# A decoder layer with 8 experts: the first expert tile filled from batches 0 to 5 only, its first layer among the routing steps

## What is computed

```python
feats = x.reshape(-1, x.shape[-1])                       # 896 x 256
scores = jax.lax.stop_gradient(feats @ centroids.T)      # 896 x 8
expert = jnp.argmax(scores, axis=1)
alpha = jax.nn.sigmoid(jnp.sum(feats * centroids[expert], axis=-1, keepdims=True))
# an expert: h = normalised xs * g + b;  xs + relu(h @ W1e.T + b1e) @ W2e.T + b2e
y = jnp.einsum('te,etd->td', onehot, ys)
out = alpha * y + (1.0 - alpha) * feats                  # then one more layer norm
```

## Time and profile before

| | |
|---|---|
| three runs | 426.25, 427.77, 428.92 us |
| the profiled execution | 426.72 us, its span 425.0 us |
| TensorE busy | 398.4 us, 94% |
| VectorE busy | 272.8 us, 64% |
| ScalarE busy | 240.8 us, 57% |
| POOL busy | 129.4 us, 30% |
| chain that ended last, by engine | TensorE 57%, VectorE 8%, ScalarE 7%, DMA 2%, POOL 1% |
| last f2 matmuls end, last L997 | 328.4 us |
| first layer of tile 0 starts | 342.2 us |
| first layer of tile 1 follows in the chain | 351.1 us |
| second layer of the last tile ends | 412.7 us |

### The profile page before, as it was taken

The page is one execution under the profiler, slowest core; times in us unless marked ns, Lnnn a source line. Parts: engine busy times, 40 slices in busy tenths (PEclk is TensorE's granted clock), DMA queues, the critical chain, the costliest instruction groups (busy, mean ns, idle before and its releaser), DMA issues.

```text
span 425.0 us, 10535 instructions
## 1 busy us (share of the span) xinstructions
PE 398.4 (94%) x3742; PEld 332.7 (78%) x3742; DVE 272.8 (64%) x944; ACT 240.8 (57%) x810; POOL 129.4 (30%) x259
## 2 busy tenths in 40 slices
PE   8989999999999999999999999999999799998980
PEld 8757787878878878787787888887889689898560
DVE  5577777777667777677776715669777737441620
ACT  0204886699787888898889986767222023324120
POOL 4250115023022231131310303324436503761421
PEclk9999999999999999999999999999999979999996
DMA  7960180610010105100000006920491421997000
GB/s 211 267 199 37 40 228 1 216 38 18 2 38 18 38 2 215 38 17 4 1 2 2 4 2 245 433 114 2 187 422 37 139 63 37 376 382 285 26 28 18
DMA packets 11561, 47.10 MB, mean 111 GB/s; under 512 B 1568, under 2 KB 6272, under 8 KB 9344
## 3 DMA queue, kind: packets, MB, share of 16 engines
q1 hardware_dynamic: 9040, 31.92, 21.9%
q0 software_dynamic: 1920, 12.35, 7.8%
q10 hardware_dynamic: 544, 2.08, 1.8%
HBM read 41.44 MB, written 4.91 MB: 109 GB/s over the span
## 4 chain that ended last, share of the span: by engine, by line
PE 57%; DVE 8%; ACT 7%; DMA 2%; issue 2%; POOL 1%; DVEq 0%; POOLq 0%; ACTq 0%
PE bank_pt L701 9%; PE bank_scores L817 6%; PE bank_out L853 5%; PE bank_out L723 5%; PE bank_out L746 5%; PE bank_pt L736 5%; PE bank_out L578 5%; PE bank_out L564 4%; PE bank_scores L685 3%; PE bank_out L571 3%; ACT arena L1286 2%; ACT arena L1297 2%; DMA arena<-expert_rows,slot_expert 2%; DVE arena L1047 1%; PE bank_scores L691 1%
## 5 line engine op out<-in xcount | busy, mean ns | idle before, releaser
L1306 ACT ACTIVATE arena<-bank_pt 125x448 f32<-125x448 f32 (+1 forms) x128 | 66.5, 546 | 34.9 <-PE bank_pt L701 34.8
L1286 ACT ACTIVATE arena<-arena,negmaxc 112x375 f32<-112x375 f32 x128 | 76.6, 604 | 13.6 <-DVE negmaxc L1047 13.2
L1047 DVE CUSTOM_DVE_ANT_0 arena<-bank_scores,arena 112x375 f32<-112x375 f32 x128 | 65.2, 543 | 18.4 <-PE bank_scores L691 12.4
L701 PE MATMUL bank_pt<-ident,arena 112*125 112x112 f32 (+1 forms) x512 | 74.7, 276 | 1.8 <-ACT arena L1306 1.2
L701 PEld LDWEIGHTS bank_pt<-ident,arena 112*125 112x125 f32 (+1 forms) x512 | 63.1, 175 | 15.0 <-ACT arena L1306 5.8
L578 PE MATMUL bank_out<-arena 128*112 128x256 f32 (+1 forms) x224 | 56.5, 383 | 0.1
L1386 POOL TENSOR_TENSOR vareps<-meanvar,scal 112x1 f32<-112x1 f32 (+1 forms) x49 | 9.5, 194 | 121.8 <-DVE meanvar L926 95.1
L1297 ACT ACTIVATE arena<-bank_scores,negmaxs 112x112 f32<-112x112 f32 x128 | 43.3, 353 | 3.4 <-DVE negmaxs L1053 2.8
L1339 ACT ACTIVATE arena<-bank_scores,consts 128x128 f32<-128x128 f32 x64 | 18.3, 369 | 45.5 <-PE bank_scores L817 41.0
L578 PEld LDWEIGHTS bank_out<-arena 128*112 128x112 f32 (+1 forms) x224 | 37.7, 181 | 7.7 <-DVE arena L977 0.5
L564 PE MATMUL bank_out<-arena 128*128 128x112 f32 x320 | 41.2, 282 | 0.2 <-DVE arena L959 0.2
(11 more groups left out here) (186 smaller groups left out, 671.1 us busy)
## 6 DMA issues: line engine op xcount, KB each, us to landing
arena<-moe SPq DMA_DIRECT2D x8, 2048.0 KB, 12.1
arena<-ctxT SPq DMA_DIRECT2D x8, 375.0 KB, 3.1
arena<-mask SPq DMA_DIRECT2D x8, 164.1 KB, 3.4
arena<-x_slots SPq DMA_DIRECT2D x9, 130.0 KB, 2.8
x_slots<-arena SPq DMA_DIRECT2D x8, 130.0 KB, 2.6
arena<-weights SPq DMA_DIRECT2D x1, 1024.0 KB, 5.2
arena<-fi SPq DMA_DIRECT2D x1, 1024.0 KB, 6.7
arena<-fo SPq DMA_DIRECT2D x1, 1024.0 KB, 8.7
```

The lines of the kernel that those rows point to most:

```text
L701: last = nc.tensor.transpose(dst[0:kp, j * S:(j + 1) * S], probs[0:S, (n % 2) * HG + j, c * kp:(c + 1) * kp], ident[0:S, 0:S])
L1047: v.tensor_tensor_reduce(out=probsC[0:S, i % (2 * HG)], in0=score_bank[j][0:S, 0:KX], in1=masks[0:S, u % 2], scale=-1.0, scalar=3.0e38, op ...
L1286: a.activation(probsC[0:S, i % (2 * HG)], probsC[0:S, i % (2 * HG)], ACT.Exp, bias=negmax["c"][0:S, u, at:at + 1], scale=-1.0, accum_out=s ...
L1306: a.activation(probsT[0:kp, n % RT, c], pt_bank[PT[stage, i] % RP][0:kp, 0:HG * S], ACT.Copy).then_inc(pt_free, 1)
```

## The change

Expert 0's tile takes rows of batches 0 to 5 only. After batch 5's ranks are made, a new step `room` raises expert 0's count to 128 if it is below (one 1x1 matmul and two operations on one element). Rows of expert 0 in batches 6 and 7 then rank beyond 128 and go to the mixed tile. The steps `xn` and `se`, the matrices `sel` and all of `WARM` are gone.

What SP reads early is now the whole tile 0. `ei` is two transposes that complete it, and its gain is two ACTIVATEs on ScalarE. New steps in the list are `tot`, the totals matmul, and `first` 0 to 7, the eight column blocks of tile 0's first layer. After the list TensorE starts with tile 0's second layer, then transposes tile 1. SP reads tiles from 1 on, and tile 0's residual comes from the early read.

`place_rest` is split: the places of the rows beyond 128 are made ahead of tile 1's normalisation, the rest (`name_parts`) after tile 0's `add_tile`. POOL sends the first two `x_more` scatters ahead of tile 0's inverse deviation. The late tiles' buffers have other places in the arena, and SP's load of the second biases waits for the last `f2` in place of the last `f1`. Most due times of the tables are changed by a little; of these the diff shows a few lines.

```diff
-FEED = [((0, 1), 33.06), ((2, 3), 37.07), ((4, 5), 42.71), ((6,), 47.72), ((7,), 51.24)]
+FEED = [((0, 1), 33.08), ((2, 3), 37.09), ((4, 5), 42.73), ((6,), 47.74), ((7,), 51.26)]
...
-FIRST_START = (-1.72, -1.37, 0.03, 1.7, 8.88, 13.57, 13.97, 19.51)
+FIRST_START = (-1.72, -1.29, 0.03, 1.76, 8.93, 13.57, 13.97, 19.52)
...
 LATE = 2
-WARM = {("sc", 6): 6, ("rk", 6): 4, ("zx", 7): 4, ("sc", 7): 4, ("rk", 7): 1}
 WARM_FIRST = 6
-HEAD = {"en": (-0.24,), "ei": (-0.24,), "xn": (-0.46, 0.34), "se": (0.14, 0.25)}
-SEND = (41.1, 44.24, 46.59, 50.31, 50.75, 53.25, 55.43, 57.33)
+HEAD = {"en": (0.21,), "ei": (-0.28,), "first": (0.41, 0.45, 0.46, 0.47, 0.48, 0.49, 0.5, 0.51), "tot": (0.39,)}
+SEND = (41.63, 44.43, 46.78, 50.45, 50.94, 53.52, 55.79, 57.94)
...
+    order.insert(min(order.index(("rk", B - LATE - 1)) + 1, order.index(("sc", B - LATE))), ("room", 0))
+    for early, later in ((("sc", B - LATE - 1), ("room", 0)), (("room", 0), ("sc", B - LATE)), (("en", 0), ("ei", 0)), (("ei", 0), ("first", 0)), (("rk", B - 1), ("tot", 0)),
+                         (("f1", FIRST_PIECE[-1] - 1), ("ei", 0)), (("sm", GROUPS - 1), ("ei", 0))):
+        assert order.index(early) < order.index(later), (early, later)
     return order
...
+        total_of = bank[5][:, 384:384 + E]
...
             sp.dma_start(xs_early, x_slots[0:128, :]).then_inc(early_in, 16)
-            sp.wait_ge(hidden_ready, FIRST_PIECE[-1])
+            sp.wait_ge(out_full, OUT["f2", B - 1] + 1)
             sp.dma_start(b2_sb.rearrange("p e d -> p (e d)"), b2rows.to_broadcast([128, E * D])).then_inc(moe_b2_in, 16)
             sp.wait_ge(out_free, N_OUT)
             sp.wait_ge(scattered, 16 * B)
             used = None
-            for t in range(TILES):
+            for t in range(1, TILES):
...
+            def first_layer(t, chunks_of=range(FC)):
+
+                w1 = moe_w[:, EXPERT_AT[t], 0:C * F].rearrange("p (c f) -> p c f", c=C)
+                for f in chunks_of:
+                    for c in range(C):
+                        last = mm(bank[2 * (t % 2) + f // 4][:, f % 4 * 128:(f % 4 + 1) * 128],
+                                  w1[:, c, f * 128:(f + 1) * 128], xsT[:, t % 2, c], start=c == 0, stop=c == C - 1)
+                    if f % 4 == 3:
+                        last.then_inc(t_hid_full, 1)
+
+            def second_layer(t):
+
+                w2 = moe_w[:, EXPERT_AT[t], C * F:].rearrange("p (f d) -> p f d", f=FC)
+                for f in range(FC):
+                    if f % 4 == 0:
+                        pe.wait_ge(t_hid_ready, 2 * t + f // 4 + 1)
+                    last = mm(bank[6 + t % 2][:, 0:D], hidT[:, t % 2, f], w2[:, f], start=f == 0, stop=f == FC - 1)
+                last.then_inc(t_y_full, 1)
+
+            def tile_transposed(j):
+
+                pe.wait_ge(t_normed, j + 1)
+                if j >= 2:
+                    pe.wait_ge(t_xT_ready, j - 1)
+                for c in range(C):
+                    last = nc.tensor.transpose(bank[4 + j % 2][:, c * 128:(c + 1) * 128],
+                                               xsn[:, j % 2, c * 128:(c + 1) * 128], ident[:, :])
+                last.then_inc(t_xT_full, 1)
...
+                elif stage == "room":
+                    pe.wait_ge(counted, 1)
+                    mm(out_slot(slot)[0:1, 0:1], chosen[0:S, B - LATE - 1, 0:1], ones[0:S, 0:1], start=True, stop=True).then_inc(out_full, 1)
                 elif stage == "ei":
-                    assert STEPS.index(("ei", 0)) < STEPS.index(("se", 0))
                     pe.wait_ge(early_normed, 1)
                     pe.wait_ge(probs_ready, PROBS["sm", GROUPS - 1] + HG)
                     for c in range(C):
-                        mm(bank[2 + c][:, 0:128], xsn_early[:, c * 128:(c + 1) * 128], ident[:, :], start=True, stop=False)
-                elif stage == "se":
-                    pe.wait_ge(late_normed, i + 1)
-                    pe.wait_ge(selected, i + 1)
-                    for c in range(C):
-                        last = mm(bank[2 + c][:, 0:128], xsn_late[:, i, c * 128:(c + 1) * 128], sel[i], start=False, stop=i == LATE - 1)
-                    if i == LATE - 1:
-                        last.then_inc(t_xT_full, 1)
-
-                for n in range(WARM.get((stage, i), 0)):
-                    if n == 0:
-                        pe.wait_ge(probs_ready, PROBS["sm", GROUPS - 1] + HG)
-                    mm(bank[0][:, 0:128], ident[:, :], ident[:, :], start=True, stop=True)
+                        last = nc.tensor.transpose(bank[2 + c][:, 0:128], xsn_early[:, c * 128:(c + 1) * 128], ident[:, :])
+                    last.then_inc(t_xT_full, 1)
+                elif stage == "tot":
+                    pe.wait_ge(hidden_ready, FIRST_PIECE[-1])
+                    pe.wait_ge(placed, B)
+                    mm(total_of, ones[0:S, :], chosen[0:S, B - 1], start=True, stop=True).then_inc(totals, 1)
+                elif stage == "first":
+                    if i == 0:
+                        pe.wait_ge(moe_in[0], 16)
+                        pe.wait_ge(t_xT_ready, 1)
+                    first_layer(0, (i,))
 
             pe.wait_ge(out_free, N_OUT)
-            pe.wait_ge(placed, B)
-
-            mm(bank[7][:, 0:E], ones[0:S, :], chosen[0:S, B - 1], start=True, stop=True).then_inc(totals, 1)
-
-
+
+            second_layer(0)
+            tile_transposed(1)
             used = None
-            for t in range(TILES):
+            for t in range(1, TILES):
                 m, halves_of = mixed(t), [bank[2 * (t % 2) + half] for half in range(2)]
 
                 if t == 5:
...
                 j = t + 1
                 if j < TILES:
                     with when_used(pe, used, j):
-
...
+                        tile_transposed(j)
                 with when_used(pe, used, t):
 
-                    if t == 1:
-                        pe.wait_ge(more_placed, 1)
                     if t >= 2:
                         pe.wait_ge(t_y_added, t - 1)
                     if m is None:
...
+                        second_layer(t)
...
-                    if i >= B - LATE:
-                        dve.wait_ge(hidden_ready, EARLY_PIECES)
-                        v.scalar_tensor_tensor(sel[i - B + LATE], slots, ebase[0:S, i:i + 1], rank[0:S, i:i + 1].to_broadcast([S, 128]),
-                                               ALU.subtract, ALU.is_equal).then_inc(selected, 1)
...
+                elif stage == "room":
+
+                    v.tensor_scalar(room[0:1], full(slot)[0:1, 0:1], -1.0, 128.0, ALU.mult, ALU.add).then_inc(out_free, 1)
+                    dve.wait_ge(out_free, slot + 1)
+                    dve.wait_ge(counted, 1)
+                    counts = chosen[0:1, B - LATE - 1, 0:1]
+                    link(v.scalar_tensor_tensor(counts, room[0:1], 0.0, counts, ALU.max, ALU.add))
                 elif stage == "en":
+
                     dve.wait_ge(early_in, 16)
                     v.tensor_scalar(xsn_early, xs_early[:, 0:D], xs_early[:, MEAN:MEAN + 1], xs_early[:, RSTD:RSTD + 1],
                                     ALU.subtract, ALU.mult).then_inc(early_normed, 1)
-                elif stage == "xn":
-                    u = B - LATE + i
-                    dve.wait_ge(hidden_ready, EARLY_PIECES)
-                    dve.wait_ge(x5_rstd, u + 1)
-                    v.tensor_scalar(xsn_late[:, i], xrows[0:S, u, 0:D], xrows[0:S, u, MEAN:MEAN + 1], xrows[0:S, u, RSTD:RSTD + 1],
-                                    ALU.subtract, ALU.mult).then_inc(late_normed, 1)
...
-            gain_tile(0)
-            normalise_tile(0)
+            v.tensor_copy(tile_token[:, 0:1], xs_early[:, TOKEN:TOKEN + 1]).then_inc(t_normed, 1)
+            place_rest()
             normalise_tile(1)
             used = None
             for t in range(TILES + 1):
                 for j, step in ((t, rows_tile), (t + 1, gain_tile), (t + 2, normalise_tile), (t - 1, finish_tile), (t, add_tile)):
-                    if t == 0 and step == add_tile:
-                        place_rest()
                     if t == 5 and step == add_tile:
                         used = parts_used(dve)
                     if 0 <= j < TILES and not (step == rows_tile and mixed(j) is None):
                         with when_used(dve, used, j):
                             step(j)
+                if t == 0:
+                    name_parts()
...
+                elif stage == "ei":
+
+                    act.wait_ge(t_xT_full, 1)
+                    for c in range(C):
+                        last = a.activation(xsT[:, 0, c], bank[2 + c][:, 0:128], ACT.Identity, bias=col("beta", c), scale=col("gamma", c))
+                    last.then_inc(t_xT_ready, 1)
...
             for t in range(E + 1):
                 if t:
                     send(t - 1)
-                inverse_deviation(t, 128, t_stats, t_rstd, t, eps=2)
+                if t:
+                    inverse_deviation(t, 128, t_stats, t_rstd, t, eps=2)
```

(3 more changed lines are left out.)

125 lines of the change are left out of this document (54 added, 71 removed), and 125 rows, old and new, of the table SHIFT.

## The result

The changed kernel takes 422.19 us, the kernel before 428.57 (medians of 20 runs each). The ratio is 0.986, interval 0.984 to 0.989: 5.8 us faster. It leaves out the executions in a slower state, three of the kernel before and two of the changed one, and so differs from the 6.4 us between the medians of all. The profiled execution took 422.64 us with a span of 420.4, where before it was 426.72 and 425.0.

The account below looks back on a forecast made before the run. Bounds: handover from routing to expert tiles, low clock there, mixed tile's parameter wait. Terms +0.2, -3.8, +1.0, -0.05 (second layer without transposes ahead), +1.1 give -1.5 us: 427.77 to 426.3, range 423.7 to 429.0.

Parts of the forecast that it names:

- From the last token_slot to tile 0's first layer: Handover from routing to tile 0: late input products and gain leave the path, 0.55 us in place of 4.37, -3.8.
- The uncovered transposes and gain of tile 1: Behind tile 0's second layer: transposes 0.22, gain and handover 0.88 no longer hidden, +1.1 us.
- The order of VectorE's steps: Last routing steps: copy and scores of batch 6 go ahead of batch 7's zf, at 331.95 instead of 330.95.
- The load of tile 1: Ahead of tile 1: load normalised at 345.6, needed at 348.4, so hidden with 2.8 us to spare.
- The stall at the mixed tile: At place 7: TensorE still stands 1.5 us for the gathered parameters, which land 1.5 us earlier.
- place_rest cost nothing: On VectorE ahead of tile 1's normalisation: place_rest, 4.0 us, is hidden behind tile 1's load.
- A part took 10.0 us ..., part 0 with none ahead of it too: Weight part gathers of later tiles: 10.0 us from issue to landing, carried over unchanged.
- rival of the stall: Mixed tile: gathers wait behind one another, so issued further apart they land sooner and TensorE does not stop; gain 3.0, chance 0.10.
- first layer 6.2 in place of 5.2, +1.0: Tile 0's first layer: 3.7 us plus 2.5 lost over 4.8 us at low clock, against 5.2 before.
- 'placed' +0.2: End of the routing steps: last token_slot at about 338.05 instead of 337.86, net +0.2 us.
- The front decides: Rival: moved steps in the first 325 us shift the time 2 us either way, 424.3 or 428.3; chance 0.15.
- A microsecond won before 351.08 is won at the end, unless something outside TensorE stops it: Expert tiles from tile 1's first layer on: about 7.25 us of TensorE each, so earlier gains carry to the end.

Follow-up runs that it names:

- a_mid: Changed kernel with tile 1's transposes between the fifth and sixth products of tile 0's second layer instead of behind it; ratio 0.982 to the kernel before.
- b_tables: Kernel before with only the changed kernel's due times for all steps up to the routing; ratio 0.998 to the kernel before.

## Why the prediction missed

**Right.** From the last token_slot to tile 0's first layer I forecast 3.8 us less: 3.65 in each of three profiles. The uncovered transposes and gain of tile 1, forecast at 1.1, were 1.13 (348.70 to 349.83), and a_mid took the wait in them away. The order of VectorE's steps made zf of batch 7 come 1.5 later, of which 0.55 was a later f2 and 1.0 the order, as forecast. The load of tile 1 was ready 1.9 us early (2.8 forecast). The stall at the mixed tile stayed (1.5 forecast; 1.28, 2.8 and 1.7 seen). place_rest cost nothing.

**A reading that was wrong.** "A part took 10.0 us ..., part 0 with none ahead of it too": the view gives 10.0 three times because it had the landing of one part only, the last. In the two further profiles of the kernel before all four are there, from 8.7 or 8.8 for the first to 9.9 or 10.5 for the last. And the parameters took 5.3 to 5.7 us with no part ahead, 8.0 to 10.1 behind the parts. So these gathers do hold each other up, against what the prediction held against its rival of the stall; the stall stayed because the parameters still followed the last part by 4.7 us, as before.

**"first layer 6.2 in place of 5.2, +1.0".** This term was mis-sized. The 6.2 rested on 4.8 us at the low clock; it was 3.3, 4.0 and 3.4, and the layer took 5.29, 5.63 and 5.39. And the 5.2 came from one profile, whose low stretch was 6.8 us; in two more it was 10.2, and the layer took 6.75 and 6.16. By the means the term is 5.4 in place of 6.0: -0.6. I took the clock "as low at 338.6" and counted the low time from there, as if it began anew. In fact the fillers' absence moved the fall to between 331 and 333, and the return came earlier with it.

**"'placed' +0.2".** It was +0.8. The missing 0.6 is the same clock: the score and rank matmuls of batch 7 ran at 0.50 (L795 and L796 took 0.54 and 0.39, in the kernel before 0.36 and 0.21), and with the fillers back the term is +0.1. I had put the low clock into the first layer only, although I said it would fall between the routing steps.

**"The front decides", chance 0.15, up to 2 us.** It gave 1.5 us (b_tables 1.7), one dip of the clock near 293 us apart, which took 1.6 back in the very profile I compared with.

**What the sum left out: the end.** "A microsecond won before 351.08 is won at the end, unless something outside TensorE stops it" holds, but the sum ended with the last second layer and took the 12.3 us behind it as fixed. This is the step that failed most: a term put at nothing without a reason. They were 9.5; in the means of three profiles each, the difference is 2.2 us of the tail and 0.4 in front of VectorE's last add, which started 0.48 us behind the matmuls in every profile of the kernels built from before and 0.11 in those of the changed kernel. The cause of the 0.4 was not tested. No rival spoke of the tail. It was in the trace of before: 8.0 us from the last scatter's issue to the end of the span, with the branches in the records, and a change that removes 47 entries from TensorE's queue could move it. That the walk over the unused code sets the tail, and that its length goes with the number of instructions, is shown. That the 2.2 us are missing from the gain once the tails are equal is not: two such pairs still differ by 7.0 and 5.7 us, the first by more at the mixed tile, the second with a stall left in the kernel before. Whether that has to do with the code taken out or is chance, one profile of each can't say.

So of the 4.3 us missed, in the means of three profiles each, 2.2 are the tail, 1.6 less lost in the first layer, 1.0 the front and 0.4 VectorE's add; against them stand 0.6 more lost ahead of placed. The rest, a start 0.6 later and the mixed tile, varies from run to run. Part of the 1.6 is chance: the low stretch of the kernel before was 3.4 us longer in two profiles than in the one that the prediction rests on.

## What to carry over

Read the stretch from the last transfer to the end of the span as its own term: where never-taken code stands at the end of an engine's program, count its long branches in the instruction records, and expect any change in the number of instructions to move them. A cost taken out of both kernels need not shrink their difference by what it was: measure the pair. Take a term that hangs on the granted clock from several profiles, since one shows only one of its lengths. And when a change pulls dense work closer to fillers, try the fillers again before removing them: here neither kept the clock alone, and together they did.

## What the hardware showed that I did not expect

- A jump over code that is not run took 0.21 us mostly and 2.0 to 3.2 us at some places, each long one with a 16384-byte instruction transfer of its own; ten entries more or fewer at the start of a queue of some 4,100 switched one of them at its end.
- With the same order and the same busy time ahead, the clock fell in one profile and not in another. It fell near 293 us in 3 of the 11 profiles with this order. These are the windows of the changed kernel's first and second profile, 3.08 of 4 us busy in both, and then 0.50 against 1.00:

```profile
288.00:292.00 4.00, 3.08 (x43) 2.37 (x42) 3.37 (x13) 2.36 (x11) 2.19 (x6) 1.00 0.00 0
292.00:294.00 2.00, 2.00 (x10) 1.96 (x11) 1.82 (x12) 0.77 (x2) 1.08 (x3) 0.50 0.01 4
```

```profile
288.00:292.00 4.00, 3.08 (x44) 2.38 (x42) 3.34 (x13) 2.51 (x11) 2.19 (x6) 1.00 0.00 0
292.00:294.00 2.00, 2.00 (x15) 1.95 (x14) 1.86 (x12) 0.62 (x2) 1.23 (x3) 1.00 0.01 4
```

- The parameters' gather of 0.9 MB took 8.0 to 10.1 us to land behind the weight parts, 5.3 to 5.7 ahead of them. Behind them, its landing set TensorE's stall: in all fourteen profiles the stall, 1.3 to 3.3 us, is the landing time less 6.7 or 6.8.
